# Order of the calls inside one pipeline step of a macaron block (attention and feed-forward, a Mamba layer between)

## The reference

```python
qkv = x @ Wqkv                       # 128 -> 3 x 16 heads x 64
q = l2norm(q) * qs; k = l2norm(k) * ksc
q = q*cos*scale + rotate_half(q)*sin*scale      # k with 1/scale
sim = einsum('bhwie,bhwje->bhwij', bq, bk2) * 8 # windows of 32, this one and the one before
attn = softmax(where(mask, -max, sim)); out = attn @ v;  x = out @ Wo + x
hg = layernorm(x) @ W1 + b1; a, gate = split(hg)
x = a * gelu(gate) @ W2 + b2 + x
```

## Time and profile before

| | before |
|---|---|
| median of 3 runs | 3296.53 us |
| the profiled execution | 3295.41 us |
| its span | 3293.6 us |
| TensorE matmul busy | 3128.0 us (95%) |
| VectorE busy | 2773.5 us (84%) |
| ScalarE busy | 2490.9 us (76%) |
| GpSimd busy | 2435.9 us (74%) |
| TensorE's share of the chain that ended last | 83% |
| granted TensorE clock, mean | 0.993 |

### The profile page before, as it was taken

How to read it: one execution, slowest core, us unless ns; L and a number is a source line. 1 busy time by engine, 2 the same in 40 slices (tenths; PEclk the granted TensorE clock), 3 DMA queues, 4 the chain that set the end, 5 groups by cost and what they waited for, 6 DMA issues and landing times.

```text
span 3293.6 us, 120453 instructions
## 1 busy us (share of the span) xinstructions
PE 3128.0 (95%) x51630; PEld 2513.7 (76%) x51630; DVE 2773.5 (84%) x3207; ACT 2490.9 (76%) x3160; POOL 2435.9 (74%) x1229
## 2 busy tenths in 40 slices
PE   7999999999999999998888999999999999999999
PEld 5887887888887887875333888888888888888777
DVE  7887888888888888876999888888888888888886
ACT  5777777777777787777676777778778777778776
POOL 6777777777777776762999868768768768768764
PEclk8999999999999999999999999999999999999999
DMA  3333333233233232231000323323323323323322
GB/s 119 88 76 86 77 85 87 72 89 87 68 92 85 70 89 66 67 76 38 26 0 0 98 67 82 88 71 85 91 69 83 95 69 81 96 66 83 73 66 68
DMA packets 142299, 245.22 MB, mean 74 GB/s; under 512 B 32397, under 2 KB 34638, under 8 KB 141774
## 3 DMA queue, kind: packets, MB, share of 16 engines
q1 hardware_dynamic: 141774, 237.51, 28.4%
HBM read 35.01 MB, written 1.05 MB: 11 GB/s over the span
## 4 chain that ended last, share of the span: by engine, by line
PE 83%; DVE 6%; issue 5%; POOL 3%; ACT 2%; DMA 0%; SPq 0%; DVEq 0%; ACTq 0%; POOLq 0%
PE PS L282 16%; PE PS L404 12%; PE PS L424 8%; PE PS L349 8%; PE PS L214 7%; PE PS L216 7%; PE PS L215 7%; PE PS L546 4%; PE PS L488 2%; PE PS L490 2%; PE PS L489 2%; PE PS L359 2%; POOL ARENA L1862 2%; PE PS L447 2%; DVE ARENA L1675 2%
## 5 line engine op out<-in xcount | busy, mean ns | idle before, releaser
L282 PE MATMUL PS<-C,ARENA 128*128 128x128 f32 x4608 | 619.7, 278 | 37.9 <-ACT ARENA L1004 11.4
L1746 POOL TENSOR_TENSOR ARENA<-ARENA 128x1024 f32<-128x1024 f32 x192 | 470.0, 2448 | 240.1 <-DVE ARENA L1325 239.2
L1754 POOL TENSOR_TENSOR ARENA<-ARENA,RN 128x1024 f32<-128x1024 f32 x192 | 365.3, 1903 | 371.4 <-ACT RN L939 371.4
L282 PEld LDWEIGHTS PS<-C,ARENA 128*128 128x128 f32 x4608 | 512.2, 141 | 119.4 <-issue 77.4
L1004 ACT ACTIVATE ARENA<-PS 64x1024 f32<-64x1024 f32 x384 | 390.5, 1017 | 181.3 <-PE PS L282 179.1
L214 PE MATMUL PS<-WL,XH 128*128 128x512 f32 x1152 | 498.8, 433 | 8.8 <-POOL XL L1713 4.0
L1740 POOL TENSOR_TENSOR ARENA<-ARENA 128x1024 f32<-128x1024 f32 x192 | 455.9, 2375 | 7.0 <-DVE ARENA L1307 7.0
L216 PE MATMUL PS<-WH,XH 128*128 128x512 f32 x1152 | 453.8, 394 | 0.0
L215 PE MATMUL PS<-WH,XL 128*128 128x512 f32 x1152 | 451.3, 392 | 0.0
L404 PE MATMUL PS<-ARENA 128*64 128x64 f32 x12288 | 402.4, 224 | 37.9 <-DVE ARENA L1365 22.2
L404 PEld LDWEIGHTS PS<-ARENA 128*64 128x64 f32 x12288 | 377.1, 138 | 72.5 <-issue 72.5
(11 more groups left out here) (160 smaller groups left out, 6454.4 us busy)
## 6 DMA issues: line engine op xcount, KB each, us to landing
ARENA<-ARENA SPq DMA_DIRECT2D x1152, 128.0 KB, 2.4
ARENA<-ARENA SPq DMA_DIRECT2D x768, 64.0 KB, 2.1
ARENA<-in_wqkv SPq DMA_DIRECT2D x36, 512.0 KB, 5.2
ARENA<-in_wo SPq DMA_DIRECT2D x12, 512.0 KB, 3.9
ARENA<-in_w SPq DMA_DIRECT2D x12, 341.0 KB, 3.2
ARENA<-in_w SPq DMA_DIRECT2D x12, 192.0 KB, 3.9
X<-in_xT SPq DMA_DIRECT2D x4, 256.0 KB, 5.5
out<-X SPq DMA_DIRECT2D x1, 768.0 KB, 3.6
```

The costliest lines, as they stand in the source:

```text
L282: last = nc.tensor.transpose(PS[:, slot, 128 * j:128 * j + 128], src[:, 128 * j:128 * j + 128], ident)
L1746: nc.gpsimd.tensor_tensor(KN[n % 2], KN[n % 2], T2, ALU.add).then_inc(k_add, 1)
```

## The change

The calls of one step are put in another order on ScalarE, VectorE and GpSimd. TensorE's order, every function's body and every wait stay as they are, and the ends of the stacks (after the loops) too. On ScalarE `exponentials` goes ahead of `ffn_high`; `split_k` behind `gelu1`; `restore_tables` ahead of `q_square`; `inverse_norms` ahead of `v_evacuate`; `split_q` ahead of `p_evacuate`; `split_input` to the end. On VectorE the gates (`gate1` now first) go ahead of `floor_sums`, and that ahead of `row_sums`; `row_max` ahead of `q_sums`; `subtract_max` ahead of `ffn_normalise`. On GpSimd `w_low_v` goes ahead of `input_low`.

```diff
@@ scalar_stack
+                exponentials(s - 20)
                 ffn_high(s - 23)
-                split_k(s - 18)
-                exponentials(s - 20)
                 q_evacuate(s - 19)
                 o_evacuate(s - 21)
                 k_evacuate(s - 19)
                 gelu0(s - 23)
                 gelu1(s - 23)
+                split_k(s - 18)
                 gelu2(s - 23)
+                restore_tables(s - 23)
                 q_square(s - 17)
+                inverse_norms(s - 18)
                 v_evacuate(s - 19)
-                restore_tables(s - 23)
-                inverse_norms(s - 18)
                 carry_evacuate(s - 18)
-                split_input(s - 24)
                 ffn_square(s - 22)
                 ffn_rsqrt(s - 22)
+                split_q(s - 17)
                 p_evacuate(s - 20)
+                split_v(s - 19)
                 k_square(s - 17)
-                split_v(s - 19)
-                split_q(s - 17)
+                split_input(s - 24)
@@ vector_stack
                 k_sums(s - 19)
+                gate1(s - 24)
+                gate0(s - 24)
+                gate2(s - 24)
+                floor_sums(s - 19)
                 row_sums(s - 21)
-                floor_sums(s - 19)
-                gate0(s - 24)
-                gate1(s - 24)
-                gate2(s - 24)
                 q_rotate1(s - 18)
                 q_rotate2(s - 18)
+                row_max(s - 20)
                 q_sums(s - 18)
                 ffn_residual(s - 24)
-                row_max(s - 20)
+                subtract_max(s - 20)
                 ffn_normalise(s - 23)
-                subtract_max(s - 20)
                 k_rotate1(s - 18)
@@ pool_stack
                 k_normalise(s - 18)
+                w_low_v(s - 19)
                 input_low(s - 24)
-                w_low_v(s - 19)
                 w_low_q(s - 17)
```

## The result

The changed kernel took 3332.45 us (median of 4 runs, 3328.26 to 3335.09), the kernel before on the same chip 3296.15 us (4 runs, 3294.58 to 3297.72). The ratio is 1.011, interval 1.0097 to 1.0122: slower by 36 us. The profiled execution took 3335.09 us with a span of 3333.3, that is 39.7 us more than the span before. The forecast was 3328 with a range of 3306 to 3346.

What follows compares the result with a forecast made beforehand. TensorE, busy 3128.0 of 3293.6 us, was the bound, with a four-engine loop 0.7 us behind in plain steps. Terms +43.2 + 1.1 + 1.5 + 3.9 - 16.5 = +33.2 on 3295.41 gave 3328 us, range 3306 to 3346.

Steps and rivals of the forecast that it cites:

- the floor's wait: VectorE's `floor_sums`, now ahead of `row_sums`, waits for GpSimd's running `k_add_halves`; `p_normalise` ends 1.40 us later.
- The loop: Four-engine loop of `p_transpose`, plain steps (feed-forward's next two): 11.8 us becomes 13.24 against TensorE's 12.47; +43.2 us.
- `split_*` "at nothing": Weight copies such as `split_v` on ScalarE: they lie in idle time and cost nothing.
- `inverse_norms` "at nothing": ScalarE, `inverse_norms` ahead of `v_evacuate`: fills an idle 0.34 us, `v_evacuate` ends 0.1 us later; no effect.
- The feed-forward steps: `subtract_max` ahead of `ffn_normalise` on VectorE removes TensorE's wait at `values`, usually 0.39 us a step: -16.5 us.
- rival 2: Feed-forward steps: the floor waits and `ffn_low` comes late, so nothing is given back; 3345 us, chance 0.13.
- The layer ends: Ten steps: `values` gains 0.66 us, then `p_transpose` meets the floor's 1.40 us; +3.9 us in all.
- Rival 3: The floor waits, but TensorE's pause lets instruction supply catch up and slow scores shrink; 3305 us, chance 0.09.
- The step ahead of the feed-forward: At least 13.42 us long, it hides the loop; only `w_low_q`, once a layer, costs: +1.5 us.
- Rival 1: The floor does not wait for GpSimd in the loop; 3272 us, faster, chance 0.08.

Runs made afterwards that it cites:

- split_v_back: The changed kernel with `split_v` put back behind `k_square` on ScalarE, nothing else: 3325.38 us, ratio 1.008 to the kernel before.
- three: The kernel before with `inverse_norms` (and table load) ahead of `v_evacuate`, `row_max` ahead of `q_sums`, `subtract_max` ahead of `ffn_normalise`: 3245.77 us, ratio 0.9845.
- floor_only: The kernel before with one move, `floor_sums` ahead of `row_sums` on VectorE: 3377.91 us, ratio 1.024.
- act_only: The kernel before with the new order of calls on ScalarE alone: 3266.22 us, ratio 0.9903.
- inv_only: The kernel before with one ScalarE move, `v_evacuate` behind `restore_tables` and `inverse_norms`: 3263.9 us, ratio 0.9893.

## Why the prediction was right, and where it was not

The side, the size and the cause were right: the floor's wait alone is worth +78 us on the kernel before, and taking it out of the change gives back 71 us by the medians (3332.45 to 3261.16), 74 by the ratios. But that the sum of 33 us came out near 36 is luck in good part: in the other terms errors of up to 10 us, of both signs, met.

**The loop.** Forecast 13.24 us and +43.2 in 82 plain steps. Measured 13.15 to 13.21 us, and +45.0 once `split_v` is out (split_v_back), +44.3 with the floor alone. The sum held to 2 us, and so did the 1.40 us by which `row_sums` moved (2.52 - 1.12). Two small errors cancel in it: the loop is about 0.1 us shorter than forecast where it runs undisturbed, and more steps than forecast are longer than the loop, 20 of the 82 at 13.4 us or more in split_v_back (3 before).

**The step that failed: `split_*` "at nothing".** The forecast placed `split_v` in idle time. Once a layer it stands ahead of `k_square`, in the very loop that the forecast had just shown to be the bound: +9.4 us in plain steps (54.4 - 45.0). Slack had been read from the trace before, where the loop had 0.7 us to spare, and not from the loop as the first term left it.

**The term that was mis-sized: `inverse_norms` "at nothing".** It is worth -36 us on the kernel before; what it is worth inside the change no run isolates. The forecast asked whether the moved instructions fit into an idle 0.34 us of ScalarE. It did not ask who waits for their result. GpSimd did, for 0.84 us, and what ends GpSimd's work sooner ends L1399 sooner. I had measured L1399's 1.43 us, had named GpSimd as its cause, and had treated it as fixed.

**The feed-forward steps.** Forecast -16.5, measured -9.7. Alone, `subtract_max` gives -20.0, so its own term was too small (it also counts 31 waits of `values` where the earlier trace rows leave 33, worth 0.1 us). Part of it is lost in the changed kernel: without the floor it is -15.0. With the floor L1399 takes 1.94 us again, though it no longer holds `subtract_max`, as foreseen. Of the 5.3 us between the two kernels 2.6 lie in four steps of the last layer and 1.6 in two other steps; in most of the others the difference is under 0.1 us. What causes it is not shown. No wait of L488 for L1773 is seen, so `ffn_low` was not late, and rival 2 did not come true.

**The layer ends.** Forecast +3.9, measured -5.9. At `values` the wait is 0.69 us, where 1.66 - 0.66 = 1.00 was forecast, and L282 then waits 1.22 for L1768:

```profile
833.93 2.09 PE L404 MATMUL PS<-ARENA 128*64 128x64 f32 x64 [0.69 <-DVE ARENA L1365]
...
842.64 0.55 PE L282 MATMUL PS<-C,ARENA 128*128 128x128 f32 x3 [1.22 <-POOL ARENA L1768]
```

The eight ordinary ends are about as forecast: 14.18 us before, 14.5 after in seven and 13.80 in one, +0.32 each against +0.65. The two ahead of the last layer fell from 18.49 and 18.32 to 14.58 and 14.54, -7.7 against -1.3. There `ffn_residual` also halves the weights W2 behind `w1_low` (L1474), which took 2.05 us before and 0.35 after:

```profile
L1474 DVE TENSOR_SCALAR ARENA<-ARENA x2: 346/346/347, 1329.7 to 3123.0; 128x384 f32<-128x384 f32 x2
```

That too is a tensor-scalar instruction that met GpSimd before and doesn't now. In the first of these ends `subtract_max` is through 2.8 us sooner after `p_transpose`, 1.7 of it from this line, where the forecast had only 0.66. It isn't the only way: in the run three L1474 still takes 2.05 us, L1283 ahead of it is short instead, and these two ends take 14.03 and 14.00 us.

**Rival 3** (TensorE's pause lets its instruction supply catch up) is not borne out. TensorE's `L349 <- issue` is 23.0 us in 50 cases before and 14.5 in 35 after, which looks like it. But two other kernels have the same pause and keep these waits: 23.9 in 53 cases in floor_only, 22.5 in 45 in split_v_back. The scores of a plain step take 1.96 us on average before, 1.95 in both of these, 1.86 after, and 1.88 in act_only, which has no pause. The step ahead of the feed-forward, forecast +1.5, became -2.5; but act_only and inv_only have -3.2 and -2.4 there without the pause, and floor_only has +4.0 with it. What moved this term is not shown.

**Rival 1** is excluded: the floor waited in the loop.

## What to carry to other kernels

Ask of every moved instruction not only whether it fits, but who waits for its result, and which instructions of other engines end with that one; "idle" beside it is not an answer. Read the slack of an edit from the schedule that the largest term leaves behind, not from the one before. Where VectorE's tensor-scalar form, or one that reads two SBUF tensors, would start under a running GpSimd instruction, look for the same result from a reduction, or for a place between two GpSimd instructions.

## What the runs showed of the hardware

- A tensor-scalar maximum over 128x32 takes 0.12 us, and 1.35 us (median) where it starts in the middle of GpSimd's `k_add_halves`; it then ends 0.03 to 0.05 us after that one. Size doesn't protect it.
- Held by a running GpSimd instruction, the 128x512 form (L1399) ends 0.28 to 0.30 us after it, the two-input L1283 0.72 to 0.73 us. That is a constant tail behind GpSimd's end, whatever the printed duration. It is shorter than the instruction's own time, which is 0.55 and 0.86 us where nothing runs beside it. So an instruction that starts in GpSimd's last 0.25 us loses nothing, as L1399 at 850.52 in inv_only, with GpSimd's end at 850.77.
- The reduction at the same place keeps its 0.22 us. The Trainium skill, "SBUF — State Buffer", section "Who interferes with whom", says that `tensor_reduce` never contends with GpSimd on this chip, and the trace agrees (201 to 223 ns in 192 cases).
- GpSimd pays as well: its `k_normalise`, which came up at a layer end of the kernel before while L1283 was running, took 2.54 us and not 1.90. It does so in 10 of the 192 cases before and in none after, where `k_normalise` is already running when L1283 comes up.

```profile
822.03 2.54 POOL L1762 TENSOR_TENSOR ARENA<-ARENA,RN 128x1024 f32<-128x1024 f32 x1
```
